# Square root as Exp of half a Ln in the score bound of an attention and expert layer (8 cores of a Trainium2)

## The chip, the cores and the metric

The program runs on the 8 cores of one Trainium2 chip, every core with its own half of one of 4 sequences. Each core has five engines that run their own queues in order: TensorE (PE, matmuls; PEld is its weight load), VectorE (DVE), ScalarE (ACT), GpSimd (POOL) and SyncE (SP). The metric is the device time in microseconds (us) of the slowest core, for one execution.

## The reference

One layer in post-norm order: self-attention with rotary positions over 4 sequences of 2048 tokens, width 2048, 16 heads of 128; then a mixture of 8 experts of which the router picks 2 per token; after both a residual sum and a layer norm. Cut to what matters:

```python
q = rotary(proj(Wq, bq)); k = rotary(proj(Wk, bk)); v = proj(Wv, bv)
attn = softmax(einsum('bhqd,bhkd->bhqk', q, k) * HD ** -0.5)
out = einsum('bhqk,bhkd->bhqd', attn, v)
x = layernorm(x + out @ Wo.T + bo)
w = sigmoid(x @ Wg.T); keep the best 2 of 8, divided by their sum
x = layernorm(x + sum_e w_e * (silu(x @ W1_e.T) * (x @ W3_e.T)) @ W2_e.T)
```

A softmax does not change when the same number is taken off all scores of a row, so any bound on the scores may stand in for their maximum.

## The kernel before, in words

Everything is kept transposed: features on the 128 partitions, tokens along the free dimension. A core has 1024 tokens of its own, and computes keys and values for all 2048 of its sequence.

The attention runs in 8 groups of 2 heads (`emit_group`). A group first makes V for both heads (L292 or L317, copied out by ScalarE at L305 or L324). Then each head goes through the same steps:

- `proj_rope` for Q (2 pieces of 512 tokens) and for K (4 pieces): 16 steps of matmuls each (L397, L403). ScalarE adds the bias (L363, Identity), VectorE squares the result (L368), a matmul with ones sums the squares (L373), and VectorE takes the largest into the small row `msc` (L377, L382, L386). The rotation itself is the "tail" of a piece: a matmul that swaps neighbours (L339) and three VectorE operations (L344, L349, L354).
- `bound_finale`, called after the last K pieces and before their two tails: VectorE multiplies the largest squared norm of Q with that of K (L430), ScalarE takes the square root, scaled (L433), a matmul with a row of ones spreads this one number over the 128 partitions (L436), and VectorE writes its negative into `mq_sb` (L439). It is the bound that the exponentials take off.
- `st_merged`: for each of 16 blocks of 128 keys two score matmuls (L472), one ScalarE exponential over 1024 scores (L479, which reads `mq_sb` as its bias), and four matmuls that sum the exponentials (L451) and weight V with them (L458). TensorE's order is L472 of block 0, L472 of block 1, L451 and L458 of block 0, L472 of block 2, and so on.
- `epilogue_m`: the division by the sum as Ln and Exp on ScalarE (L491, L495), a VectorE product (L499) and the V bias (L503).

After the 8 groups come the output projection (L542) with the residual and the statistics of the first layer norm, the router, the eight experts (L782, L799, L856) and the second layer norm.

The order of the work is that of the code: each engine replays its own list, and `Sched` gives every operation a semaphore wait on the last writer or the readers of what it uses. Operations on the same engine wait on each other in the same way, except on TensorE. The loads of ScalarE's function tables (ACT_TABLE_LOAD) do not stand in the code: they are put in when the program is compiled, and the profile gives them the line of the operation that they stand in front of.

Of the kernel before, what the change touches and what calls it, by code (L numbers as in the profile page):

```python
# [7 lines left out]
AF = mybir.ActivationFunctionType  # L8
# [13 lines left out]
SCALE = float(HD) ** -0.5  # L22
# [101 lines left out]
def build_program(debug=False):  # L124
# [62 lines left out]
    msc = nc.alloc_sbuf_tensor("msc", [1, 8], F32)  # L187
# [26 lines left out]
    def T(fn, r=(), w=()):  # L214
        S_.op("tensor", fn, r, w)

    def V(fn, r=(), w=()):
        S_.op("vector", fn, r, w)

    def A(fn, r=(), w=()):  # L220
        S_.op("scalar", fn, r, w)
# [26 lines left out]
    for dc in range(NDC):  # L248
        G(lambda g, dc=dc: g.dma_start(
            R1_bf.ap()[:, dc * S:(dc + 1) * S], d_x[dc]),  # L250
            r=([f"R1_{dc - 2}"] if dc >= 2 else []),
            w=[f"R1_{dc}"], dma=f"gx{dc % 2}")
# [3 lines left out]
        w=["ws0", "ws1"], dma="swq")  # L256
# [4 lines left out]
        w=["ws2", "ws3"], dma="swk")  # L261
    G(lambda g: g.dma_start(
        wg_sb.ap().rearrange("p (dc e) -> p dc e", dc=NDC), d_wg),
        w=["wg"], dma="gld")
    T(lambda t: t.matmul(pa[0].ap()[:, 0:NE], ones_r_f.ap(), fbrow.ap(),
                         start=True, stop=True),
      r=["ones", "fbrow"], w=["pa0"])
    V(lambda v: v.tensor_copy(fbb.ap(), pa[0].ap()[:, 0:NE]),
      r=["pa0"], w=["fbb"])

    def emit_group(gi):
        if gi > 0:
# [7 lines left out]
                w=["ws0", "ws1"], dma="swq")  # L280
# [4 lines left out]
                w=["ws2", "ws3"], dma="swk")  # L285

        if gi == 0:
            for dc in range(NDC):
                def vmm0(t, dc=dc):
# [13 lines left out]
                  w=[f"pa{b}" for b in range(8)])  # L303
            for tc in range(NDC):
# [3 lines left out]
                    r=[f"pa{tc // 2}"], w=[f"vb{tc}"])  # L308
        else:
            for tc in range(NDC):  # L310
# [3 lines left out]
                def vmm(t, tc=tc, bank=bank):  # L314
# [11 lines left out]
                    r=[pk], w=[f"vb{tc}"])  # L326

        for hl in range(2):
# [100 lines left out]
            def bound_finale():  # L429
                V(lambda v: v.tensor_tensor(  # L430
                    msc.ap()[0:1, 6:7], msc.ap()[0:1, 4:5], msc.ap()[0:1, 5:6],
                    ALU.mult), r=["msc"], w=["msc"])
                A(lambda s: s.activation(msc.ap()[0:1, 7:8], msc.ap()[0:1, 6:7],  # L433
                                         AF.Sqrt, scale=SCALE * SCALE),
                  r=["msc"], w=["msc"])
                T(lambda t: t.matmul(  # L436
                    pa[3].ap()[:, 0:1], ones_r_f.ap(), msc.ap()[0:1, 7:8],
                    start=True, stop=True), r=["msc", "ones"], w=["pa3"])
                V(lambda v: v.tensor_scalar(  # L439
                    mq_sb.ap()[:, 6:7], pa[3].ap()[:, 0:1], -1.0, None,  # L440
                    ALU.mult), r=["pa3"], w=["mq"])

            proj_rope(4, 4096 + hl * 2048, ["ws2" if hl == 0 else "ws3"], bkc,
                      "bkc", ck_sb, sk_sb, kbuf, koff,
                      [f"kb{hl}_{i}" for i in range(4)], finale=bound_finale)

            def st_merged():
# [64 lines left out]
    for gi in range(NH // 2):  # L512
        emit_group(gi)
        if debug and gi == 0:
            Y(lambda s: s.dma_start(d_dbg_qkv[0][:, 0:2 * TL], qbuf.ap()),
              r=["qb0_0", "qb0_1", "qb1_0", "qb1_1"], dma="dbg5")
            Y(lambda s: s.dma_start(d_dbg_qkv[1], kbuf.ap()),
              r=[f"kb{h}_{i}" for h in range(2) for i in range(4)], dma="dbg5")
            Y(lambda s: s.dma_start(d_dbg_qkv[2], vbuf.ap()),
              r=[f"vb{t}" for t in range(NDC)], dma="dbg5")  # L520

    for i in range(NDC):
        V(lambda v, i=i: v.tensor_copy(
            xy.ap()[:, i * TL:(i + 1) * TL], R1_bf.ap()[:, i * S: i * S + TL]),
            r=[f"R1_{i}"], w=[f"xy{i}"])

    if debug:
        Y(lambda s: s.dma_start(d_dbg_ao, aog.ap()),
          r=[f"ao{h}" for h in range(NH)], dma="dbg6")
    pending_stats = [None]  # L530
    for ec in range(NHC):
# [5 lines left out]
            w=[wok], dma=f"swo{sl}")  # L537
# [15 lines left out]
        for nq in range(2):  # L553
# [5 lines left out]
                r=[f"pa{ob + nq}", f"xy{ec}", "boc"], w=[f"R1_{ec}"])  # L559
# [97 lines left out]
    for nq in range(2):  # L657
        V(lambda v, nq=nq: v.tensor_copy(
            scr_f.ap()[0:8, nq * 512:(nq + 1) * 512], pa[nq].ap()[0:8, :]),
            r=[f"pa{nq}"], w=["sf0", "sf1"])  # L660
    for tt in range(8):
# [5 lines left out]
            r=["pa2"], w=["rt"])  # L667
    A(lambda s: s.activation(wr_sb.ap(), rt_sb.ap(), AF.Sigmoid),
      r=["rt"], w=["wr"])
# [4 lines left out]
    for tt in range(8):  # L674
# [26 lines left out]
      r=["m1"], w=["m1"])  # L701
# [180 lines left out]
    for e in range(NE):  # L882
        emit_h13(e, hook=lambda e=e: emit_ew_rows(e))
        emit_w2(e, stats=(e == NE - 1))
        if debug:
            Y(lambda s, e=e: s.dma_start(d_dbg_acc[e], R1_f32.ap()),
              r=[f"R1_{i}" for i in range(NHC)], dma="dbg2")
            Y(lambda s, e=e: s.dma_start(d_dbg_g[e], aog.ap()),
              r=[f"ao{j}" for j in range(NH)], dma="dbg3")
            Y(lambda s, e=e, sl=e % 2: s.dma_start(  # L890
                d_dbg_ewb[e], scr_f.ap()[:, sl * TL:(sl + 1) * TL]),
                r=[f"sf{2 * (e % 2)}", f"sf{2 * (e % 2) + 1}"], dma=f"dbg4{e % 2}")
# [118 lines left out]
```

How the kernel before makes its waits and increments, by code:

```python
    def replay(self, engname, engobj):  # L103
        wm = {}
        for o in self.stream[engname]:
            waits = {}
            for d in o["deps"]:
                if d["cnt"] is None:
                    continue
                val = (self.totals[d["sem"]]
                       if (d["dma"] and d["dma"] in self.batch_sems)
                       else d["cnt"])
                if waits.get(d["sem"], 0) < val:
                    waits[d["sem"]] = val
            wl = [(k, v) for k, v in waits.items() if wm.get(k, 0) < v]
            for k, v in wl:
                engobj.wait_ge(self.handles[k], v)
                wm[k] = v
            inst = o["fn"](engobj)
            if o["marked"]:
                inst.then_inc(self.handles[o["sem"]], 16 if o["dma"] else 1)
# [798 lines left out]
        @block.sync  # L920
        def _(s):
            S_.replay("sync", s)
            s.wait_ge(handles[("dma", "st")], st_total)
```

## Time and profile before

| what | us |
|---|---|
| the two timed runs | 3157.67 and 3518.6 |
| their median | 3338.14 |
| the profiled execution | 3156.6 |
| its span, on the slowest core (core 7) | 3155.1 |
| the spans of the eight cores | 3143.8 to 3155.1 |
| busy in that span: PE | 2631.6 (83%) |
| DVE | 802.7 (25%) |
| ACT | 637.3 (20%) |
| POOL | 172.2 (5%) |

The span runs from the first to the last instruction of the program on the slowest core, and the rows below are of that core. A busy time adds what an engine worked anywhere in the span; it says nothing of who waited. Matmuls are pipelined, so the busy time of PE counts more than the array's work. The granted clock is the share of TensorE's full 2.4 GHz that the chip allowed in a stretch; 0.50 is 1.2 GHz.

### The profile page before, as it was taken

To read this page: it belongs to the slowest core of one execution; us is meant where nothing else is said; L and a number is where in the kernel's file an instruction comes from. 1 tells how busy PE (TensorE), PEld (TensorE's weight loads), DVE (VectorE), ACT (ScalarE), POOL (GpSimd) and SP (SyncE) were. 2 spreads that over 40 slices of the span, in tenths; PEclk is the share of its full clock that TensorE was granted. 3 is DMA by queue.
4 is the path that set the end of the run, shared out by engine and by line. 5 is a ranking of instruction groups with operands and counts; after the bars stand their busy time and mean duration, and the time that the engine had idled before them with its cause. 6 is when DMAs were issued, how large, how long until landed. Compare 5 with 4: busy or idle time off the path is not lost.

```text
span 3155.1 us, 32027 instructions; the slowest of 8 cores (3143.8 to 3155.1 us)
## 1 busy us (share of the span) xinstructions
PE 2631.6 (83%) x12262; PEld 1205.3 (38%) x12262; DVE 802.7 (25%) x1452; ACT 637.3 (20%) x824; POOL 172.2 (5%) x323
## 2 busy tenths in 40 slices
PE   4777777878777777779849999998989999998993
PEld 3234242524243342424314344343434444343441
DVE  0222223121312222222271212213131222213126
ACT  0342424334333324243200000000000000000031
POOL 1000000000000000000000101001010100101000
PEclk9888898988888888989969999999999999999996
DMA  9210101001000101002403444344444444444423
GB/s 152 37 27 14 27 14 27 14 14 26 15 14 14 27 14 27 8 7 47 81 14 67 70 70 74 61 80 61 75 70 70 74 67 77 61 77 62 73 44 117
DMA packets 50726, 155.32 MB, mean 49 GB/s; under 512 B 6162, under 2 KB 6290, under 8 KB 49298
## 3 DMA queue, kind: packets, MB, share of 16 engines
q0 software_dynamic: 47264, 142.69, 27.8%
q1 hardware_dynamic: 3314, 10.59, 0.9%
q8 instruction: 101, 1.65, 0.2%
q14 instruction: 47, 0.39, 0.0%
HBM read 287.54 MB, written 8.39 MB: 94 GB/s over the span
## 4 chain that ended last, share of the span: by engine, by line
PE 73%; DVE 9%; DMA 9%; issue 5%; ACT 4%; DVEq 0%; ACTq 0%; POOL 0%; POOLq 0%
PE pb L782 14%; PE pb L799 14%; PE pb L856 9%; DMA wslab<-w_t 6%; PE pb L317 6%; PE pb L397 6%; PE pb L403 6%; PE pb L451 4%; PE pb L458 3%; PE pb L542 3%; PE pb L472 3%; DMA R_bf<-x_t 2%; PE pb L373 1%; DVE scr_bf L368 1%; ACT scr_bf L479 1%
## 5 line engine op out<-in xcount | busy, mean ns | idle before, releaser
L856 PE MATMUL pb<-aog,wslab 128*128 128x512 bf16 x2048 | 459.6, 380 | 56.1 <-DMA wslab<-w_t 55.5
L782 PE MATMUL pb<-xy,wslab 128*128 128x512 bf16 x2048 | 464.8, 386 | 0.0
L799 PE MATMUL pb<-xy,wslab 128*128 128x512 bf16 x2048 | 452.5, 379 | 0.0
L793 ACT ACTIVATE scr_bf<-pb 128x512 bf16<-128x512 f32 x128 | 69.5, 594 | 1321.3 <-PE pb L782 1321.3
L856 PEld LDWEIGHTS pb<-aog,wslab 128*128 128x128 bf16 x2048 | 194.7, 98 | 317.3 <-issue 97.4
L397 PE MATMUL pb<-R_bf,wslab 128*128 128x512 bf16 x768 | 311.0, 405 | 5.5 <-ACT vbuf L305 5.5
L403 PE MATMUL pb<-R_bf,wslab 128*128 128x512 bf16 x768 | 310.1, 404 | 0.0
L479 ACT ACTIVATE scr_bf<-pb,mq_sb 128x1024 bf16<-128x1024 f32 x256 | 283.4, 1114 | 103.5 <-PE pb L472 103.3
L782 PEld LDWEIGHTS pb<-xy,wslab 128*128 128x128 bf16 x2048 | 202.5, 99 | 251.4 <-issue 19.0
L799 PEld LDWEIGHTS pb<-xy,wslab 128*128 128x128 bf16 x2048 | 200.5, 98 | 241.5
L869 DVE TENSOR_TENSOR R_f<-pb,R_f 128x512 f32<-128x512 f32 x256 | 177.1, 692 | 340.6 <-PE pb L856 327.3
L814 DVE TENSOR_TENSOR scr_bf<-pb,scr_f 128x512 bf16<-128x512 f32 x128 | 88.0, 687 | 646.7 <-PE pb L799 646.7
L451 PE MATMUL pb<-scr_bf,ones_sq 128*128 128x512 bf16 x512 | 205.6, 402 | 26.3 <-ACT scr_bf L479 15.7
L317 PE MATMUL pb<-wslab,R_bf 128*128 128x256 bf16 x1792 | 209.6, 282 | 14.7 <-ACT vbuf L324 14.7
L458 PE MATMUL pb<-scr_bf,vbuf 128*128 128x512 bf16 x512 | 204.8, 400 | 0.0
L373 PE MATMUL pb<-scr_bf,ones_sq 128*128 128x512 bf16 x96 | 41.7, 435 | 192.8 <-DVE scr_bf L368 191.1
L317 PEld LDWEIGHTS pb<-wslab,R_bf 128*128 128x128 bf16 x1792 | 180.7, 101 | 43.9 <-issue 16.5
L472 PE MATMUL pb<-qbuf,kbuf 128*128 128x512 bf16 x512 | 173.9, 425 | 19.2 <-DVE scr_f L344 19.2
L368 DVE TENSOR_TENSOR scr_bf<-scr_bf 128x512 bf16<-128x512 bf16 x96 | 40.4, 420 | 411.4 <-ACT scr_bf L363 411.4
L499 DVE TENSOR_TENSOR aog<-pb,scr_f 128x512 bf16<-128x512 f32 x32 | 22.1, 692 | 431.0 <-ACT scr_f L495 431.0
L363 ACT ACTIVATE scr_bf<-pb,bkc 128x512 bf16<-128x512 f32 x64 | 42.3, 686 | 388.0 <-DVE scr_f L349 219.4
L397 PEld LDWEIGHTS pb<-R_bf,wslab 128*128 128x128 bf16 x768 | 79.5, 103 | 107.4 <-issue 29.8
(116 smaller groups left out, 1585.5 us busy)
## 6 DMA issues: line engine op xcount, KB each, us to landing
wslab<-w_t POOLq DMA_DIRECT2D x128, 512.0 KB, 5.1
wslab<-w_t POOLq DMA_DIRECT2D x128, 256.0 KB, 3.8
wslab<-wv_t POOLq DMA_DIRECT2D x8, 1024.0 KB, 9.0
R_bf<-x_t POOLq DMA_DIRECT2D x16, 512.0 KB, 7.0
wslab<-wq_t POOLq DMA_DIRECT2D x8, 1024.0 KB, 9.4
wslab<-wk_t POOLq DMA_DIRECT2D x8, 1024.0 KB, 9.4
wslab<-wo_t POOLq DMA_DIRECT2D x16, 512.0 KB, 5.0
y<-R_f SPq DMA_DIRECT2D x16, 512.0 KB, 2.6
```

What stands on the lines that cost most here:

```text
L317: last = t.matmul(pa[bank].ap()[:, 0:256], R1_bf.ap()[:, dc * S + tc * 128: dc * S + tc * 128 + 128], wslab.ap()[:, 8192 + dc * 256: 8192 ...
L397: t.matmul(pa[pb[0]].ap(), wslab.ap()[:, wbase + dc * 128: wbase + dc * 128 + 128], R1_bf.ap()[:, dc * S + a * 512: dc * S + a * 512 + 512 ...
L403: return t.matmul(pa[pb[1]].ap(), wslab.ap()[:, wbase + dc * 128: wbase + dc * 128 + 128], R1_bf.ap()[:, dc * S + a * 512 + 512: dc * S + ...
L451: T(lambda t, kc=kc, j=j, qb=qb: t.matmul(pa[6 + qb].ap(), ones_sq.ap(), scr_bf.ap()[:, j * 1024 + qb * 512: j * 1024 + qb * 512 + 512], s ...
L458: T(lambda t, kc=kc, j=j, qb=qb, hl=hl: t.matmul(pa[4 + qb].ap(), vbuf.ap()[:, kc * 256 + hl * 128: kc * 256 + hl * 128 + 128], scr_bf.ap( ...
L472: t.matmul(pa[2 * j + qb].ap(), kbuf.ap()[:, koff + kc * 128: koff + kc * 128 + 128], qbuf.ap()[:, qoff + qb * 512: qoff + qb * 512 + 512] ...
L479: A(lambda s, j=j: s.activation(scr_bf.ap()[:, j * 1024:(j + 1) * 1024], pb[j].ap(), AF.Exp, bias=mq_sb.ap()[:, 6:7], scale=SCALE), r=[f"p ...
L542: last = t.matmul(pa[ob + nq].ap(), wslab.ap()[:, sl * 2048 + dc * 128: sl * 2048 + dc * 128 + 128], aog.ap()[:, dc * TL + nq * 512: dc * ...
L782: last = t.matmul(pa[nc2].ap(), wslab.ap()[:, W1OFF[s1] + dc * 128: W1OFF[s1] + dc * 128 + 128], xy.ap()[:, dc * TL + nc2 * 512: dc * TL + ...
L799: last = t.matmul(pa[4 + nc2].ap(), wslab.ap()[:, W3OFF[s1] + dc * 128: W3OFF[s1] + dc * 128 + 128], xy.ap()[:, dc * TL + nc2 * 512: dc * ...
L856: last = t.matmul(pa[wb + nc2].ap(), wslab.ap()[:, W2OFF[s2] + fc * 128: W2OFF[s2] + fc * 128 + 128], aog.ap()[:, fc * TL + nc2 * 512: fc ...
L869: V(lambda v, hc=hc, nc2=nc2, wb=wb: v.tensor_tensor(R1_f32.ap()[:, hc * TL + nc2 * 512: hc * TL + nc2 * 512 + 512], pa[wb + nc2].ap(), R1 ...
```

## The change

In `bound_finale` the one ScalarE instruction that took the square root becomes two: a Ln with the same scale, and an Exp of half of it, which reads and writes the same single number. exp(ln(x) / 2) is the square root of x. Nothing else is changed. The lines behind it move down by three in the changed kernel.

```diff
                 A(lambda s: s.activation(msc.ap()[0:1, 7:8], msc.ap()[0:1, 6:7],
-                                         AF.Sqrt, scale=SCALE * SCALE),
+                                         AF.Ln, scale=SCALE * SCALE),
+                  r=["msc"], w=["msc"])
+                A(lambda s: s.activation(msc.ap()[0:1, 7:8], msc.ap()[0:1, 7:8],
+                                         AF.Exp, scale=0.5),
                   r=["msc"], w=["msc"])
```

ScalarE's queue in one head before, from the K pieces to the first half of the epilogue (the waits in brackets are the semaphores of the engines named):

```order
L363 ACTIVATE scr_bf<-pb,bkc 128x512 [waits e_tensor,e_scalar,e_vector] x2
L433 ACTIVATE msc<-msc 1x1 [waits e_vector]
L479 ACTIVATE scr_bf<-pb,mq_sb 128x1024 [waits e_tensor,e_vector]
L479 ACTIVATE scr_bf<-pb,mq_sb 128x1024 [waits e_tensor,e_vector,e_scalar]
L479 ACTIVATE scr_bf<-pb,mq_sb 128x1024 [waits e_tensor,e_scalar] x14
L491 ACTIVATE scr_f<-pb 128x512 [waits e_tensor]
L495 ACTIVATE scr_f<-scr_f 128x512 [waits e_scalar]
```

The one ScalarE instruction between the K pieces and the exponentials is L433. Here is the same place in the changed kernel, where L482, L494 and L498 are the L479, L491 and L495 of before:

```order
L363 ACTIVATE scr_bf<-pb,bkc 128x512 [waits e_tensor,e_scalar,e_vector] x2
L433 ACTIVATE msc<-msc 1x1 [waits e_vector]
L436 ACTIVATE msc<-msc 1x1 [waits e_scalar]
L482 ACTIVATE scr_bf<-pb,mq_sb 128x1024 [waits e_tensor,e_vector] x2
L482 ACTIVATE scr_bf<-pb,mq_sb 128x1024 [waits e_tensor,e_scalar] x14
L494 ACTIVATE scr_f<-pb 128x512 [waits e_tensor]
L498 ACTIVATE scr_f<-scr_f 128x512 [waits e_scalar]
```

One instruction is added, the new L436, and it waits for the one in front of it on its own engine. Nothing changes places.

## Rows read from the trace of the kernel before

**Rows 1.** The chain that ended last, share of the span by engine.

```profile
PE 73%; DVE 9%; DMA 9%; issue 5%; ACT 4%; DVEq 0%; ACTq 0%; POOL 0%; POOLq 0%
```

**Rows 2.** ScalarE's groups: count | busy us, mean ns | idle before, until whom.

```profile
L324 ACT CAST vbuf<-pb 128x256 bf16<-128x256 f32 x112 | 40.9, 371 | 149.8 <-PE pb L317 149.8
...
L479 ACT ACT_TABLE_LOAD x16 | 20.5, 1283 | 43.2 <-DVE scr_f L349 43.2
...
L495 ACT ACTIVATE scr_f<-scr_f 128x512 f32<-128x512 f32 x32 | 20.1, 629 | 3.2 <-ACT scr_f L491 0.4
L433 ACT ACT_TABLE_LOAD x15 | 19.2, 1283 | 68.1 <-DVE msc L430 68.1
L491 ACT ACTIVATE scr_f<-pb 128x512 f32<-128x512 f32 x32 | 18.8, 588 | 9.9 <-PE pb L451 9.9
...
L433 ACT ACTIVATE msc<-msc 1x1 f32<-1x1 f32 x16 | 3.2, 202 | 5.3 <-DVE msc L430 5.1
...
L305 ACT ACT_TABLE_LOAD x1 | 1.3, 1283 | 79.5 <-PE pb L292 79.5
```

**Rows 3.** Waits: engine, line <- whom: us in total, times, longest.

```profile
ACT L433 <- DVE msc L430: 68.1, 15, 4.8
...
PE pb L436 <- ACT msc L433: 47.9, 16, 3.1
```

**Rows 4.** Timeline, first head: start, us, engine, line [idle before <- releaser].

```profile
128.39 0.15 DVE L430 TENSOR_TENSOR msc<-msc 1x1 f32<-1x1 f32 x1
128.62 0.20 ACT L433 ACTIVATE msc<-msc 1x1 f32<-1x1 f32 x1 [5.09 <-DVE msc L430]
...
128.97 0.55 PE L436 MATMUL pb<-msc,ones_r_f 1*128 1x1 f32 x2 [1.79 <-ACT msc L433]
```

**Rows 5.** Timeline, second head, from its L430 to its first L451 and L458.

```profile
199.02 0.15 DVE L430 TENSOR_TENSOR msc<-msc 1x1 f32<-1x1 f32 x1
199.25 1.28 ACT L433 ACT_TABLE_LOAD   x1 [4.46 <-DVE msc L430]
200.54 0.20 ACT L433 ACTIVATE msc<-msc 1x1 f32<-1x1 f32 x1
...
200.89 0.55 PE L436 MATMUL pb<-msc,ones_r_f 1*128 1x1 f32 x2 [3.07 <-ACT msc L433]
...
203.43 1.28 ACT L479 ACT_TABLE_LOAD   x1 [2.69 <-DVE scr_f L349]
...
204.09 0.68 DVE L344 TENSOR_TENSOR scr_f<-pb,sk_sb 128x512 f32<-128x512 f32 x1
...
204.73 2.12 ACT L479 ACTIVATE scr_bf<-pb,mq_sb 128x1024 bf16<-128x1024 f32 x2
...
204.92 0.58 PE L472 MATMUL pb<-qbuf,kbuf 128*128 128x512 bf16 x1 [1.20 <-DVE scr_f L344]
...
205.98 0.58 PE L451 MATMUL pb<-scr_bf,ones_sq 128*128 128x512 bf16 x1 [0.47 <-ACT scr_bf L479]
...
206.37 0.63 PE L458 MATMUL pb<-scr_bf,vbuf 128*128 128x512 bf16 x1
...
206.79 0.63 PE L451 MATMUL pb<-scr_bf,ones_sq 128*128 128x512 bf16 x1
```

**Rows 6.** Timeline, second head, Ln and Exp of its epilogue.

```profile
229.47 0.60 ACT L491 ACTIVATE scr_f<-pb 128x512 f32<-128x512 f32 x1 [0.62 <-PE pb L451]
...
230.16 0.63 ACT L495 ACTIVATE scr_f<-scr_f 128x512 f32<-128x512 f32 x1
```

**Rows 7.** Stretches: length, busy PE, PEld, DVE, ACT, POOL (counts), granted clock, DMA share, GB/s.

```profile
818.16:827.17 9.01, 5.62 (x14) 1.95 (x15) 4.03 (x7) 4.89 (x5) 0.00 (x0) 0.50 0.00 0
827.17:848.43 21.26, 20.18 (x89) 7.53 (x88) 0.00 (x0) 16.16 (x15) 0.00 (x0) 1.00 0.00 1
1164.75:1175.33 10.58, 7.18 (x17) 2.40 (x18) 4.04 (x8) 5.78 (x6) 0.00 (x0) 0.50 0.00 0
1175.33:1195.79 20.46, 19.23 (x85) 7.28 (x84) 0.00 (x0) 15.26 (x15) 0.00 (x0) 1.00 0.00 1
```

## The prediction

> **What bounds the kernel now.** I read the chain of work that ended last first, then the ScalarE groups, then the waits, then the timeline of two heads. The chain's summary gives PE 73% of the span and ACT 4% [rows 1]: TensorE sets the time, and ScalarE counts only where TensorE stands still for it. The ScalarE groups show where the changed line matters [rows 2]: an ACT_TABLE_LOAD of 1283 ns belongs to L433 15 times and to L479 16 times, one pair in each of the 16 heads, except that the first head has no L433 load. So ScalarE loads the table that has Sqrt, runs one 1x1 Sqrt of 202 ns, and loads another table for the softmax exponentials. Nothing else loads a table inside the attention: Ln (L491) and Exp (L495), the copies (L324) and the biased Identity (L363) run between these loads without one. L305's single load, before the first head, is the table in which the first Sqrt is already found. In all, 31 loads stand in the attention, 20.5 + 19.2 = 39.7 us of ScalarE time; what they are worth is decided by who waits for them.
>
> The waits [rows 3] say that TensorE stood 47.9 us before L436 until ACT L433, 16 times, 3.1 us the longest. That stretch begins while VectorE still reduces the maxima, so not all of it is the load. Two heads part the two: the first head runs the same chain without a load. There L430 starts at 128.39, the Sqrt at 128.62 and L436 at 128.97, which is 0.58 us from L430 to L436 [rows 4]. In the next head L430 starts at 199.02, the load at 199.25, the Sqrt at 200.54 and L436 at 200.89, which is 1.87 us [rows 5]. The L433 load costs the chain 1.87 - 0.58 = 1.29 us, its full length: ScalarE's queue waits for L430 first and loads after it.
>
> **The change, part by part.** (a) Sqrt becomes Ln. Ln and Exp follow each other at L491 and L495 with no load between them, and the second starts 0.09 us after the first ends (229.47 + 0.60 to 230.16) [rows 6]. If one table with Ln, Exp, Identity and the copy is in place from L305 on, the 15 loads of L433 go, and nothing in this chain hides them: 1.29 us a head. A 1x1 Ln I price like the 1x1 Sqrt, 202 ns [rows 2], so the swap itself is worth nothing.
>
> (b) The Exp is added. It needs the Ln's result and lies on the same chain in front of L436, with 202 ns for the instruction and 0.09 us for the wait between dependent ScalarE operations: 0.29 us a head, in all 16. Bounds: 0.20 us if the two overlapped fully at the seam, 0.72 us if the Exp took as long as L495's 128x512 one (629 ns + 0.09) [rows 2]; I take 0.29, because the 1x1 row is the same size. Behind the Ln and the Exp on ScalarE's queue stands only L479's first exponential, which needs L472's scores, and these are behind L436 on TensorE anyway. On TensorE the two swap products L339 and all of L472 queue behind L436; on VectorE the L344 to L354 tail queues behind L439. So the whole head moves with L436.
>
> (a) and (b) together: 1.29 - 0.29 = 1.00 us earlier in 15 heads, 0.29 us later in the first.
>
> (c) The 16 loads in front of L479's first exponential go too. This one is partly covered. In [rows 5] the load runs from 203.43 to 204.71, the first two exponentials follow from 204.73, and TensorE's L451 starts at 205.98 when the first is done. Without the load the first exponential would start at 203.43 and end some 1.06 us later (two take 2.12), near 204.5. But L451 stands behind the fourth L472 in TensorE's order, and that starts at 204.92, released by VectorE's L344 (L344 of 204.09 frees the bank that it writes). Matmuls there start 0.42 us apart (L458 at 206.37, L451 at 206.79), so L451 can start at 204.92 + 0.42 = 205.34 at the earliest. The gain is 205.98 - 205.34 = 0.64 us, not 1.28; what is late next is VectorE's L344. Bounds: 0 if something else holds L451, 1.28 if L472 too came forward. I take 0.64 in each of 16 heads.
>
> Raw sum: 15 x (1.00 + 0.64) + (0.64 - 0.29) = 24.6 + 0.35 = 24.95 us, say 25.0.
>
> (d) TensorE's clock takes part of this back. Around each of these stalls the granted clock is 0.50 (1.2 GHz), and it comes back to full only some way into the score loop. Two heads show what the moment of return is worth [rows 7], each followed from the end of L430 to the end of its last L458. In one, the half-speed stretch lasts 9.01 us and the full-speed rest 21.26, 30.27 in all; in the other 10.58 and 20.46, 31.04 in all. So 1.57 us more of half speed costs 0.77 us, about half. If the clock returns at the same moment as now although the work starts earlier, the work pulled forward runs at half speed and only about half of the 25.0 is kept, 12.5 us. If the return moves with the work, all 25.0 stay. Nothing in the trace of before fixes which; it will differ from head to head as the heads shift against these moments. I take the middle, 18.8 us. The Trainium skill (TensorE: Matmul & The Clock Gate, Part 1) says that the monitor behind this clock runs freely and is not started by the work, which speaks against the full gain. By that rule alone, in a head whose return stays put, the sum would be 12.5; by the row alone either end is possible.
>
> (e) A second rule of the Trainium skill (ScalarE: Activation LUTs, What ACT_TABLE_LOAD costs) makes a switch dearer: about 2.66 us, of which 1283 ns are the load and the rest a drain. The load agrees with the 1283 ns of [rows 2]; the drain is not seen, since the chain with a load is longer by 1.29 us in all. By the page's price the 15 switches at L433 would be worth another 15 x 1.37 = 20.6 us, and the time would be 3117.2. TensorE's wait leaves no room for it: the first head's 1.79 us [rows 4] taken 16 times and 15 x 1.29 for the loads make 48.0 us, and 47.9 were measured [rows 3]. So the rows decide, and this case gets no chance of its own.
>
> The rest of the program (projection of the output, both layer norms, the eight experts) keeps its instructions and merely starts earlier.
>
> The profiled execution took 3156.6 us for a span of 3155.1; the sum is made against the former: 3156.6 - 18.8 = 3137.8. Of the two timed runs the lower, 3157.67, agrees with it within 1.1 us; the median, 3338.14, is the middle between it and a run of 3518.6, and is not what the forecast is compared with.
>
> **The rivals.** (1) Everything removed counts: the L479 load in full, the clock moving with the work. 15 x (1.00 + 1.28) + 0.99 = 35.2, so 3121.4. For it: the load does lie straight in front of the exponential. Against it: the fourth L472, which waits for VectorE [rows 5].
> (2) The L479 load turns out to be worth nothing and the clock keeps half of the rest: (15 x 1.00 - 0.29) / 2 = 7.4, so 3149.2. For it: L472's wait for L344 ends 0.2 us after the load does. Against it: L451 starts 0.64 us after L472 would let it.
> (3) The other side: Ln and Exp are served from different tables. Then each head keeps a load in front of the Ln, gets a second 1.28 us load between Ln and Exp, and loses only the one before L479: 1.28 + 0.29 - 0.64 = 0.93 us worse per head, 14.9 us over 16, so 3171.5. It decides as soon as one load stands between the two 1x1 instructions. For it: the trace of before never shows this short pair. Against it: L491 and L495 alternate 32 times without a load [rows 2, 6], and 15 us is the most that it costs.
> (4) The change doesn't do what it says: the loads at L433 and L479 stay as they are, because the first table is chosen for another function, and only the Exp is added: 16 x 0.29 = 4.6 us, so 3161.2.
>
> **How the numbers follow.** My forecast 0.72, rival 1 0.09, rival 2 0.12, rival 3 0.05, rival 4 0.02. The forecast's own ends are 3131.6 (all of 25.0) and 3144.1 (half of it). To leave out no more than 2 in 10, the range reaches down near rival 1 and up to rival 2: 3122 to 3149. A change of 2% is 63 us, about what a measurement of this kernel can tell from none; the largest case here is 35 us. So within 2% gets 0.96; 0.02 on either side is for what shifts later, such as the waits for expert weights.
>
> **What would show it.** Right: of the loads in the attention only that of L305 remains; the new pair takes about 0.2 us each with no gap above 0.1; the wait of TensorE for the new Exp falls from 47.9 us to about 47.9 - 15.00 + 0.29 = 33.2; the first exponential starts as soon as its two score products are done; L451 follows the fourth L472 without a gap. Wrong: any load between the 1x1 instructions (rival 3), a gap in front of L451 that remains (c), or heads that end 1.64 us earlier each with no part given back, or less than half of it (d).

## The result, and the profile after

| | before | changed |
|---|---|---|
| timed executions, median | 3204.34 (18 runs) | 3138.44 (19 runs) |
| ratio, with its 95% interval | | 0.9912 [0.9887, 0.9936] |
| once more, beside the last experiments | 3162.64 (11 runs) | 3141.18 (6 runs), 0.9938 [0.9924, 0.9951] |
| profiled execution | 3156.6 | 3135.5 |
| spans of the eight cores, mean | 3150.7 | 3131.6 |

Some executions of either kernel come out up to 12% longer at a lower granted clock on a part of the cores; they are in the medians, and the ratios are taken without them.

The changed kernel is faster, by 0.6 to 0.9%. The two intervals share 0.9924 to 0.9936, which is 20 to 24 us, and the profiled executions are 21.1 us apart. The gain was forecast as 18.8 us of 3156.6, a ratio of 0.9940, which lies just outside the first interval and inside the second. The time itself came within 0.6 us of the forecast (3138.44 against 3137.8), which is luck: the section on why the prediction was right or wrong names the errors that cancel in it.

The chain that ended last, by engine, in the changed kernel:

```profile
PE 73%; DVE 9%; DMA 9%; issue 6%; ACT 3%; DVEq 0%; ACTq 0%; POOL 0%; POOLq 0%
```

ScalarE's share falls from 4% to 3% [rows 1]. Its groups (line, engine, operation, count | busy us, mean ns | idle before, until whom):

```profile
L433 ACT ACTIVATE msc<-msc 1x1 f32<-1x1 f32 x16 | 3.2, 202 | 73.8 <-DVE msc L430 73.8
L436 ACT ACTIVATE msc<-msc 1x1 f32<-1x1 f32 x16 | 3.2, 202 | 1.5
...
L305 ACT ACT_TABLE_LOAD x1 | 1.3, 1283 | 82.3 <-PE pb L292 82.3
L671 ACT ACT_TABLE_LOAD x1 | 1.3, 1283 | 45.4 <-DVE rt_sb L668 45.4
L796 ACT ACT_TABLE_LOAD x1 | 1.3, 1283 | 7.0 <-PE pb L785 7.0
L608 ACT ACT_TABLE_LOAD x1 | 1.3, 1283 | 6.2 <-DVE scr_f L604 6.2
```

The 31 loads at L433 and L479 of [rows 2] are gone. One load at L305 serves all of the attention, and the three others stand outside it. The new Exp (L436) takes the same 202 ns as the Ln, and ScalarE idles 1.5 us before it in all, 0.09 us each time: no load between the two.

The waits that answer to [rows 3]:

```profile
ACT msc L433 <- DVE msc L430: 73.8, 16, 5.0
...
PE pb L439 <- ACT msc L436: 33.5, 16, 2.1
...
PE pb L475 <- DVE scr_f L344: 19.2, 16, 1.2
```

TensorE's wait for the bound falls from 47.9 to 33.5 us; 33.2 was forecast. The wait that now holds the first sum, L475 for VectorE's L344 (the L472 of before), is 19.2 us in 16 heads. The second head in order of time, against [rows 5] (the slowest core is now core 3, so the clock of the rows is shifted):

```profile
197.62 0.15 DVE L430 TENSOR_TENSOR msc<-msc 1x1 f32<-1x1 f32 x1
197.86 0.20 ACT L433 ACTIVATE msc<-msc 1x1 f32<-1x1 f32 x1 [4.47 <-DVE msc L430]
198.16 0.20 ACT L436 ACTIVATE msc<-msc 1x1 f32<-1x1 f32 x1
...
198.50 0.55 PE L439 MATMUL pb<-msc,ones_r_f 1*128 1x1 f32 x2 [2.09 <-ACT msc L436]
...
201.06 1.11 ACT L482 ACTIVATE scr_bf<-pb,mq_sb 128x1024 bf16<-128x1024 f32 x1 [2.70 <-DVE scr_f L349]
...
201.71 0.68 DVE L344 TENSOR_TENSOR scr_f<-pb,sk_sb 128x512 f32<-128x512 f32 x1
...
202.54 0.59 PE L475 MATMUL pb<-qbuf,kbuf 128*128 128x512 bf16 x1 [1.20 <-DVE scr_f L344]
...
202.91 0.63 PE L454 MATMUL pb<-scr_bf,ones_sq 128*128 128x512 bf16 x1
...
203.34 0.63 PE L461 MATMUL pb<-scr_bf,vbuf 128*128 128x512 bf16 x1
```

From L430 to the spreading matmul it is 0.88 us (198.50 - 197.62) where it was 1.87. The first exponential starts at 201.06 with no load in front of it, when VectorE's L349 releases it, and L454 follows the fourth score product after 0.37 us (202.54 to 202.91), where L451 started 1.06 us behind it before. From L430 to the first sum it is 5.29 us, where it was 6.96.

For the comparisons below I use three numbers, each a mean over the eight cores. S adds up, over the 16 heads, the time from the start of L430 to the start of the first sum of exponentials: it is the part that the edits change directly. T is the time from the end of the first L430 to the first matmul of the output projection: all of the attention from the first head's bound on. H is the time in T at half clock, added up from the granted clock of the trace. Each comes from one traced execution of a kernel. Before: S 110.3, T 1307.6, H 304.0. Changed: S 84.7, T 1285.3, H 283.6; traced once more, beside the last experiments, it gave 84.7, 1285.4 and 284.6. So S fell by 25.6 us and T by 22.3. The mean span fell by 19.1: what lies before and behind T is 3.2 us longer, of which 2.7 are the eight experts and the layer norm behind them (1536.1 to 1538.8, with single cores between 1529.6 and 1541.0 in the two traces). That part has the same code in all kernels, and it took between 1535.9 and 1539.3 us in the other traces without extra matmuls, so the 2.7 us lie within its spread and are not shown to be a cost of the change.

### The profile page after: what moved, and what is told of

It reads as the page before. It is cut to its first block, busy times and chain, and to the rows that moved or that the text cites. A ratio compares the mean times of both kernels' runs of the same rounds, so it can differ in the third digit from the quotient of the medians.

```text
span 3134.0 us, 32012 instructions; the slowest of 8 cores (3128.2 to 3134.0 us)
## 1 busy us (share of the span) xinstructions
PE 2629.3 (84%) x12262; PEld 1206.9 (39%) x12262; DVE 802.2 (26%) x1452; ACT 602.5 (19%) x809; POOL 172.3 (5%) x323
## 4 chain that ended last, share of the span: by engine, by line
PE 73%; DVE 9%; DMA 9%; issue 6%; ACT 3%; DVEq 0%; ACTq 0%; POOL 0%; POOLq 0%
PE pb L785 14%; PE pb L802 14%; PE pb L859 9%; DMA wslab<-w_t 6%; PE pb L397 6%; PE pb L403 6%; PE pb L317 6%; PE pb L454 4%; PE pb L475 4%; PE pb L461 4%; PE pb L545 4%; DMA R_bf<-x_t 2%; DVE scr_f L344 1%; PE pb L373 1%; DVE scr_bf L368 1%
## 5 line engine op out<-in xcount | busy, mean ns | idle before, releaser
L482 ACT ACTIVATE scr_bf<-pb,mq_sb 128x1024 bf16<-128x1024 f32 x256 | 285.1, 1114 | 163.7 <-PE pb L475 119.7
L454 PE MATMUL pb<-scr_bf,ones_sq 128*128 128x512 bf16 x512 | 209.5, 409 | 18.8 <-ACT scr_bf L482 9.5
L317 PE MATMUL pb<-wslab,R_bf 128*128 128x256 bf16 x1792 | 202.9, 276 | 15.3 <-ACT vbuf L324 15.3
L373 PE MATMUL pb<-scr_bf,ones_sq 128*128 128x512 bf16 x96 | 41.9, 437 | 192.7 <-DVE scr_bf L368 191.1
L317 PEld LDWEIGHTS pb<-wslab,R_bf 128*128 128x128 bf16 x1792 | 177.4, 99 | 41.1 <-issue 17.0
L475 PE MATMUL pb<-qbuf,kbuf 128*128 128x512 bf16 x512 | 177.0, 432 | 19.2 <-DVE scr_f L344 19.2
L397 PEld LDWEIGHTS pb<-R_bf,wslab 128*128 128x128 bf16 x768 | 79.0, 103 | 103.4 <-issue 25.0
L403 PEld LDWEIGHTS pb<-R_bf,wslab 128*128 128x128 bf16 x768 | 79.0, 103 | 101.4 <-issue 20.5
```

What stands on the lines that cost most here:

```text
L317: last = t.matmul(pa[bank].ap()[:, 0:256], R1_bf.ap()[:, dc * S + tc * 128: dc * S + tc * 128 + 128], wslab.ap()[:, 8192 + dc * 256: 8192 ...
L397: t.matmul(pa[pb[0]].ap(), wslab.ap()[:, wbase + dc * 128: wbase + dc * 128 + 128], R1_bf.ap()[:, dc * S + a * 512: dc * S + a * 512 + 512 ...
L403: return t.matmul(pa[pb[1]].ap(), wslab.ap()[:, wbase + dc * 128: wbase + dc * 128 + 128], R1_bf.ap()[:, dc * S + a * 512 + 512: dc * S + ...
L454: T(lambda t, kc=kc, j=j, qb=qb: t.matmul(pa[6 + qb].ap(), ones_sq.ap(), scr_bf.ap()[:, j * 1024 + qb * 512: j * 1024 + qb * 512 + 512], s ...
L475: t.matmul(pa[2 * j + qb].ap(), kbuf.ap()[:, koff + kc * 128: koff + kc * 128 + 128], qbuf.ap()[:, qoff + qb * 512: qoff + qb * 512 + 512] ...
L482: A(lambda s, j=j: s.activation(scr_bf.ap()[:, j * 1024:(j + 1) * 1024], pb[j].ap(), AF.Exp, bias=mq_sb.ap()[:, 6:7], scale=SCALE), r=[f"p ...
```

## The experiments

**The load in front of the exponentials alone (e1_hoist).** The kernel before, with one instruction more:

```diff
...
+                A(lambda s: s.activation(dum.ap(), ones_r_f.ap()[0:1, 0:1], AF.Exp),
+                  r=["ones"], w=["dum"])
```

> The kernel before, with one more ScalarE instruction, a 1x1 Exp into an unused number, right behind the Sqrt and off the chain: the load of the exponentials' table then falls into ScalarE's wait for the scores, while the Sqrt keeps its own load on the chain. This is part (c) alone. Measure: from the start of the first L430 to that of the last, mean of the eight cores (1277.2 us before, 1255.4 after). Theory (c), 0.64 us in each of 15 heads, 9.6 us raw: 1267.6 if all of a shift is kept, 1270.0 if three quarters, 1272.4 if the clock keeps half. Rival, that load is hidden behind VectorE anyway: 1277. Rival, it counts in full (1.28): 1258.

Ratio 0.9988 [0.9951, 1.0025]. From the first to the last L430 1273.8 us, a smaller gain than even the case in which half is kept; S 99.2, T 1304.1, H 308.7. The timeline of its second head (lines are one or three further down than before):

```profile
198.66 0.15 DVE L431 TENSOR_TENSOR msc<-msc 1x1 f32<-1x1 f32 x1
198.89 1.28 ACT L434 ACT_TABLE_LOAD   x1 [4.67 <-DVE msc L431]
200.18 0.20 ACT L434 ACTIVATE msc<-msc 1x1 f32<-1x1 f32 x1
200.40 1.28 ACT L437 ACT_TABLE_LOAD   x1
...
200.53 0.55 PE L439 MATMUL pb<-msc,ones_r_f 1*128 1x1 f32 x2 [3.08 <-ACT msc L434]
...
201.70 0.20 ACT L437 ACTIVATE dum<-ones_r_f 1x1 f32<-1x1 f32 x1
...
203.09 1.11 ACT L482 ACTIVATE scr_bf<-pb,mq_sb 128x1024 bf16<-128x1024 f32 x1 [1.19 <-DVE scr_f L350]
...
204.56 0.59 PE L475 MATMUL pb<-qbuf,kbuf 128*128 128x512 bf16 x1 [1.20 <-DVE scr_f L345]
...
204.94 0.63 PE L454 MATMUL pb<-scr_bf,ones_sq 128*128 128x512 bf16 x1
```

The load behind the Sqrt now stands at 200.40, beside the spreading matmul, and nobody waits for it. The first exponential starts when VectorE's L350 (the L349 of before) releases it (203.09), and the first sum is held by the fourth score product (204.56) as part (c) said: S falls by 11.1 us, 0.69 per head for the 0.64 of (c). Yet T falls by 3.5 only. H rose by 4.7.

**The chain alone (e4_chain_only).** The changed kernel, with a 1x1 Sqrt off the chain behind the Exp, which brings the load in front of the first exponential back:

```diff
...
+                A(lambda s: s.activation(dum.ap(), ones_r_f.ap()[0:1, 0:1], AF.Sqrt),
+                  r=["ones"], w=["dum"])
```

> The changed kernel with one more ScalarE instruction, a 1x1 Sqrt into an unused number behind the Exp and off the chain: the chain to the spreading matmul stays short as in the changed kernel, but the load in front of the first exponential is back. This is parts (a) and (b) without (c), the other half of e1_hoist. The stretch from the start of L430 to the first sum of exponentials, added over 16 heads, was 110.3 us before, 99.2 in e1_hoist and 84.7 in the changed kernel; here 95.5 is expected. Measure: first L430 to the output projection, mean of the cores: 1307.6 before, 1304.1 in e1_hoist, 1285.3 in the changed kernel. If a fixed share of a shift is kept (87%, as between before and changed): 1294.7. If what is kept depends on where the heads come to lie against the moments at which the clock returns, there is no such share, and anything between 1303 and 1288 can come (the 31% of e1_hoist to the 126% of f1_late_spread).

Ratio 0.9964 [0.9952, 0.9977]. S 95.9 as expected, T 1297.0, H 295.0: 10.6 of 14.4 us kept, neither the 87% nor an extreme. The two halves alone are worth 3.5 and 10.6 us of T, 14.1 together; both at once are worth 22.3. The parts do not add up, though their S does (11.1 + 14.4 = 25.5, and 25.6 together).

**A longer chain (e2_pad4, e3_pad12).** The changed kernel with four or twelve more 1x1 instructions on the chain:

```diff
+                for _ in range(4):              # 12 in e3_pad12
+                    A(lambda s: s.activation(msc.ap()[0:1, 7:8], msc.ap()[0:1, 7:8],
+                                             AF.Identity), r=["msc"], w=["msc"])
```

> The changed kernel with four more 1x1 Identity instructions on the chain between the Exp and the spreading matmul. Each is 0.20 us and a wait of 0.09 as the Exp was priced, so 1.16 us a head and 17.4 us over the 15 heads between the first and the last L430 (1255.4 us in the changed kernel, mean of the cores). If a shift of the work is kept whole: 1272.8. If three quarters, as part (d) chose: 1268.5. If half: 1264.1. It tests the price of (b) per instruction too: L430 to the spreading matmul should grow by 1.16 us.

> The same with twelve Identity instructions, 3.48 us a head, 52.2 us over the 15 heads, more than one step of the moments at which the clock returns. If a shift is kept whole in the mean: 1307.6. Three quarters: 1294.6. Half: 1281.5.

Ratios 1.0025 [1.0015, 1.0034] and 1.0112 [1.0095, 1.0129]. From first to last L430 1274.7 and 1311.6 us. S grew by 18.8 and 56.9, T by 19.8 and 59.2: about all of the delay arrives, and the even share of three quarters fails. In e2_pad4 one core lifts the mean: core 0 took 1316.3 us in T, the seven others 1303.3 to 1303.6, which is 18.2 longer than the changed kernel. TensorE's wait in e2_pad4:

```profile
PE pb L442 <- ACT msc L440: 52.2, 16, 3.3
```

It was 33.5, so 16 x 4 instructions cost 18.7 us there, 0.29 each, the price of part (b).

**Without the Exp (e5_no_exp).** The changed kernel less its second instruction.

```diff
-                A(lambda s: s.activation(msc.ap()[0:1, 7:8], msc.ap()[0:1, 7:8],
-                                         AF.Exp, scale=0.5),
-                  r=["msc"], w=["msc"])
```

> The changed kernel without the added Exp: the bound is then the Ln alone, so the exponentials and the output are not the reference's; the instructions are otherwise the same. It prices part (b) by itself. L430 to the spreading matmul, 0.88 us in the changed kernel, should fall to 0.59, as in the first head of before, and the 16 stretches from L430 to the first sum by 4.7 us (84.7 to 80.0). First L430 to the output projection, 1285.3 in the changed kernel: 1280.6 if all of it is kept, 1283 if half; by the sum of half the change of these stretches and half the change of the half-speed time in between (283.6 us in the changed kernel), which met all runs so far within 1.2 us, whatever that half-speed time turns out to be.

```profile
PE pb L436 <- ACT msc L433: 28.8, 16, 1.8
```

The Exp costs 33.5 - 28.8 = 4.7 us of TensorE's wait, and S is 80.0, 4.7 less, as expected. T is 1277.6: 7.7 us less for 4.7 taken away, more than the case in which all is kept (1280.6). H is 275.0, 8.6 less. Ratio to before 0.9916 [0.9899, 0.9932].

**The bound spread later (f1_late_spread).** The two swap products L339 go in front of the spreading matmul, which takes a bank of its own, and VectorE's negation goes between the two tails (shortened, with comments added):

```diff
-                emit_tail(nt - 2)
-                emit_tail(nt - 1)
...
+                    emit_tail(nt - 2, "t")
+                    emit_tail(nt - 1, "t")
+                    spread()                    # the matmul of L436, into pa[5]
+                    emit_tail(nt - 2, "v")
+                    neg()                       # VectorE's L439
+                    emit_tail(nt - 1, "v")
...
```

> The changed kernel with the spreading matmul behind the two swap products in TensorE's order, into another bank, and VectorE's negation between the two tails, so that the tails of K run while ScalarE works on the bound. L430 to the first L454-like sum of exponentials was 5.14 us; VectorE's L344 of the second tail, which holds the fourth score product, can start some 1.5 us earlier, so about 3.6 us and 1.5 x 15 = 23 us raw from first to last L430: 1232 if the shift is kept whole, 1238 at three quarters, 1244 at half. Rival: TensorE's wait for ScalarE was covered by VectorE's tails anyway: 1255.

Ratio 0.9836 [0.9821, 0.9850]. From first to last L430 1228.5 us, more than the whole shift. S 61.0, T 1255.4, H 247.1: S fell by 23.7 against the changed kernel, T by 29.9. Its second head:

```profile
196.06 0.15 DVE L442 TENSOR_TENSOR msc<-msc 1x1 f32<-1x1 f32 x1
196.16 0.69 DVE L348 TENSOR_TENSOR scr_f<-pb,sk_sb 128x512 f32<-128x512 f32 x1
...
196.59 0.20 ACT L448 ACTIVATE msc<-msc 1x1 f32<-1x1 f32 x1
...
196.94 0.55 PE L453 MATMUL pb<-msc,ones_r_f 1*128 1x1 f32 x2 [1.24 <-ACT msc L448]
...
198.17 0.15 DVE L458 TENSOR_SCALAR mq_sb<-pb 128x1 f32<-128x1 f32 x1
198.24 0.68 DVE L348 TENSOR_TENSOR scr_f<-pb,sk_sb 128x512 f32<-128x512 f32 x1
198.61 2.30 ACT L499 ACTIVATE scr_bf<-pb,mq_sb 128x1024 bf16<-128x1024 f32 x2 [1.82 <-PE pb L492]
...
199.06 0.58 PE L492 MATMUL pb<-qbuf,kbuf 128*128 128x512 bf16 x1 [0.18 <-DVE scr_f L348]
...
199.87 0.58 PE L471 MATMUL pb<-scr_bf,ones_sq 128*128 128x512 bf16 x1 [0.22 <-ACT scr_bf L499]
```

VectorE's L348 (the L344 of before) starts 0.10 us behind L442 (the L430), beside ScalarE's Ln and Exp, and the first sum comes 3.81 us behind the start of L442 (3.66 behind its end, from which the expected 3.6 was counted).

**Two moves more (f2_scores_first).** In f1_late_spread, the first two score products go ahead of the spreading matmul and both L344 products ("swap" below) ahead of the negation:

```diff
+                for qb in range(2):             # the scores of block 0, then
+                    T(lambda t, ...: t.matmul(pa[qb].ap(), ...))
                 T(lambda t: t.matmul(pa[5].ap()[:, 0:1], ones_r_f.ap(), ...))
...
+                    emit_tail(nt - 2, "swap")
+                    emit_tail(nt - 1, "swap")
                     neg()
```

> f1_late_spread with two more moves: TensorE's first two score products go in front of the spreading matmul, and VectorE's two L344 products go in front of the negation, so that the fourth score product no longer waits for the whole first tail. L430 to the first sum was 3.81 us in f1_late_spread and should come to about 3.1, as the first exponential then starts some 1.9 us behind L430 and takes 1.1: 16 x 0.7 = 11 us less in these stretches (61.0 to 50). First L430 to the output projection, 1255.4 in f1_late_spread: 1244 if all is kept, 1250 if half. If the first exponential waits for something else, 1255.

Ratio 0.9807 [0.9792, 0.9821], the fastest kernel of the study that adds no work; its median is 3100.45 us against 3162.64 for before. S 48.9 (50 expected), T 1248.1, H 245.1: 7.3 of 12.1 us kept. Two of its waits:

```profile
ACT scr_bf L510 <- DVE mq_sb L469: 17.0, 16, 1.1
...
PE pb L464 <- ACT msc L453: 6.2, 16, 0.4
```

TensorE's wait for the bound, 47.9 us before and 33.5 in the changed kernel, is 6.2.

**Extra matmuls that hold the clock (w1_warm_before, w2_warm_after, w3_warm_late).** To the kernel before, the changed one and f1_late_spread, matmuls are added in front of the L373 products and of the spreading matmul:

```diff
+    def warm(n):
+        def wmm(t):
+            for i in range(n):
+                last = t.matmul(pa[5].ap(), ones_sq.ap(), R1_bf.ap()[:, 0:512],
+                                start=True, stop=True)
+            return last
+        if n:
+            T(wmm, r=["R1_0", "ones"], w=["pa5"])
...
+                    warm(18 if nq == 2 else 6)
...
+                warm(8)
```

The 8 in front of the spreading matmul are those of w2_warm_after; w1_warm_before has 12 and w3_warm_late 2.

> The kernel before, with extra matmuls on ones whose result nobody reads, into a free bank, in the stretches in which TensorE waits in a head: 18 in front of the third L373 of K, 6 in front of each other L373, 12 in front of the spreading matmul. They are there to keep TensorE's clock at full through the head. If the half-speed clock costs what the comparison of the runs says (about half of the work's length in half-speed stretches), some 3 to 5 us a head go: first L430 to the output projection 1307.6 falls to about 1230 to 1260. If the extra matmuls only lie in the way, it rises by up to 16 x 2 = 32.

> The changed kernel with the same extra matmuls (8 in front of the spreading matmul, whose wait is shorter). Against w1_warm_before this is the change without the clock: with the clock full in both, the difference of the two from first L430 to the output projection should equal the difference of their stretches from L430 to the first sum of exponentials within 2 us, that is all of it is kept, some 28 us (1.0 us for the chain and about 0.85 for the load in front of the exponentials in each head, where matmuls at full clock stand 0.22 us apart). If a shift is given back for another reason than the clock, less than 24.

> f1_late_spread with the extra matmuls (2 in front of the spreading matmul): both gains in one kernel. If they add, f1_late_spread's 1255.4 us from first L430 to the output projection falls by what w2_warm_after gains over the changed kernel, by an estimate 40 to 70 us. If f1_late_spread already took most of what the clock costs, by under 30.

T is 1252.4, 1219.7 and 1211.4 us, S 97.8, 75.6 and 57.8. The stretch T of w2_warm_after on its slowest core (length, busy us of PE, PEld, DVE, ACT, POOL with counts, granted clock, DMA share, GB/s):

```profile
128.95:1350.92 1221.97, 1117.56 (x5741) 554.20 (x5823) 307.32 (x593) 447.54 (x581) 14.18 (x22) 0.99 0.11 19
```

The granted clock there is 0.99. That the half-speed clock costs the attention tens of us is shown: 55 us go from before to w1_warm_before, although it has more matmuls. But the clean comparison failed: in w1_warm_before 71.3 us of T are still at half clock and in w2_warm_after 29.0, so the two differ by 32.7 us for 22.2 of S. The profiled executions are 3118.79, 3085.04 and 3071.72 us. The ratios are 0.9857 [0.9842, 0.9872] for w1_warm_before and 0.9721 [0.9706, 0.9736] for w3_warm_late; none came out for w2_warm_after. Over all their executions the medians of w2_warm_after and w3_warm_late are 3233.25 and 3252.61 us against 3162.18 for before, so I do not call them an improvement. The experts and the layer norm behind them, with the same code, took 1547.3 to 1549.7 us in these three against 1536.1 before; what the extra matmuls do there was not tried. The gains of f1_late_spread and of the matmuls add only in part: 1255.4 falls by 44.0 us, within the 40 to 70 expected, but the changed kernel's T falls by 65.6.

## Why the prediction was right or wrong

**Parts (a), (b), (c) and their sum: right.** The 15 loads at L433 were on the chain in full (1.87 to 0.88 us, 0.99 a head against 1.00 forecast), the Exp costs 0.29 (e2_pad4 and e5_no_exp measure it twice), and the load in front of the first exponential is worth 0.69 (e1_hoist) instead of 0.64, held by VectorE's L344 as named. The raw sum was 25.0; S fell by 25.6. One sign did not hold: the first exponential does not start with its score products but when VectorE's L349 releases it, as [rows 5] showed already. It cost nothing, since the fourth score product comes later. Taking the load off the chain gave 0.99 + 0.29 = 1.28 us, its own length. The further drain that the Trainium skill (ScalarE: Activation LUTs, What ACT_TABLE_LOAD costs) counts with a switch shows nowhere here.

**Part (d), what the clock gives back: the step that failed.** It said that half to all of the shift is kept, took the middle, 75%, and looked for the clock's answer only in the stretch around the bound. Measured: 22.3 of 25.6 us, 87%, 3.5 us more than the forecast 18.8. T splits into the heads (from the start of each L430 to the end of its last sum of exponentials; 493.4 us before, 475.3 changed) and what lies between them (814.2 and 810.0). The heads kept 18.1 us, 71%: there the middle was close. The other 4.2 us were gained between the heads, where the time at half clock fell from 80.2 to 69.1 us a core; (d) put any change there at nothing. So the term was mis-sized by what it left out, and its two ends were wrong too, as the other pairs of kernels show:

| from, to | S | H | T | (S + H) / 2 | T / S | T in the heads | T between them |
|---|---|---|---|---|---|---|---|
| before, e1_hoist | -11.1 | +4.7 | -3.5 | -3.2 | 32% | -10.0 | +6.5 |
| before, e4_chain_only | -14.4 | -9.0 | -10.6 | -11.7 | 74% | -11.1 | +0.5 |
| before, changed | -25.6 | -20.4 | -22.3 | -23.0 | 87% | -18.1 | -4.2 |
| changed, e5_no_exp | -4.7 | -8.6 | -7.7 | -6.7 | 164% | -6.8 | -0.9 |
| changed, e2_pad4 | +18.8 | +20.0 | +19.8 | +19.4 | 105% | +12.2 | +7.6 |
| changed, e3_pad12 | +56.9 | +59.9 | +59.2 | +58.4 | 104% | +57.4 | +1.8 |
| changed, f1_late_spread | -23.7 | -36.5 | -29.9 | -30.1 | 126% | -36.9 | +7.1 |
| f1_late_spread, f2_scores_first | -12.1 | -2.0 | -7.3 | -7.1 | 60% | -6.7 | -0.5 |
| w1_warm_before, w2_warm_after | -22.2 | -42.3 | -32.7 | -32.3 | 147% | -39.8 | +7.1 |

There is no fixed share: the same kind of edit keeps a third of its time in one place and half as much again in another. The column (S + H) / 2 is bookkeeping. Time at half clock is stall plus work, and work there takes twice as long (in the second head of before, whose half-speed stretch ends at 209.36, 128x512 matmuls start 0.42 us apart at half clock, 208.93 to 209.35, and 0.22 apart at full, 209.57 to 209.79; the lines follow). So a change costs its stall and half of the change in work done at half clock, which is (H - S) / 2. It meets T within 1.1 us in all nine pairs, and so nothing but the stall and the clock is needed to explain T. One trace shows the same with no edit at all: in e2_pad4, core 0 has the S of the other seven within 0.1 us, 26.3 us more H than core 1, and 12.7 us more T, nearly all of it between the heads. So T differs by some us between cores that run the same instructions, and a share of a small shift such as e5_no_exp's 4.7 us is rough. The sum is not a forecast, since H is known only from the trace of the new kernel.

```profile
208.93 0.60 PE L458 MATMUL pb<-scr_bf,vbuf 128*128 128x512 bf16 x1
209.35 0.39 PE L451 MATMUL pb<-scr_bf,ones_sq 128*128 128x512 bf16 x1
209.57 0.38 PE L458 MATMUL pb<-scr_bf,vbuf 128*128 128x512 bf16 x1
209.79 0.59 PE L472 MATMUL pb<-qbuf,kbuf 128*128 128x512 bf16 x2
```

How the clock gives back and adds is seen in the second head. Here is the half-speed stretch around the bound in the kernel before (columns as in [rows 7]):

```profile
195.71:209.36 13.65, 7.38 (x18) 2.37 (x19) 6.21 (x13) 5.39 (x6) 0.00 (x0) 0.50 0.34 59
```

In the changed kernel, with the stretches around it:

```profile
185.00:194.62 9.62, 4.81 (x22) 1.91 (x20) 4.46 (x8) 1.37 (x2) 0.71 (x1) 1.00 0.21 37
194.62:208.27 13.65, 9.15 (x22) 3.28 (x23) 5.96 (x13) 3.75 (x5) 0.00 (x0) 0.50 0.34 53
208.27:220.00 11.73, 11.58 (x50) 4.21 (x49) 0.00 (x0) 9.06 (x9) 0.00 (x0) 1.00 0.00 0
```

In e1_hoist:

```profile
194.42:208.07 13.65, 7.51 (x18) 2.61 (x19) 6.37 (x14) 5.40 (x7) 0.00 (x0) 0.50 0.30 60
208.07:220.00 11.93, 11.60 (x52) 4.33 (x51) 0.00 (x0) 9.38 (x9) 0.00 (x0) 1.00 0.00 0
```

And in f1_late_spread:

```profile
191.66:201.90 10.24, 6.58 (x15) 2.07 (x16) 6.39 (x14) 2.63 (x4) 0.00 (x0) 0.50 0.56 95
```

The stretch is 13.65 us long in all three of the first kernels: in the changed kernel the stall got shorter, the stretch did not, and TensorE ran 22 matmuls in it instead of 18. The four more cost about 0.2 us each, out of the 1.67 us that this head gained. In f1_late_spread the stretch is 10.24 us and holds 15 matmuls. All heads of all cores (8 x 16) together, from the granted clock in the traces:

| kernel | half-speed stretch around the bound, us | other half-speed stretches in T |
|---|---|---|
| before | 13.65 in 106 heads, 17.07 in 22 | 188 |
| e1_hoist | 13.65 in 128 | 206 |
| e4_chain_only | 13.65 in 128 | 188 |
| changed | 13.65 in 128 | 160 |
| e5_no_exp | 13.65 in 115, 10.24 in 13 | 154 |
| e2_pad4 | 13.65 in 128 | 204 |
| e3_pad12 | 17.07 in 128 | 169 |
| f1_late_spread | 10.24 in 128 | 204 |
| f2_scores_first | 10.24 in 128 | 200 |

Two things decide what a shorter stall is worth. The first is the stretch around the bound, which had one of three lengths and did not slide along with the work by the tenths of a us that an edit moves it. What its end is worth is what (d) read off two heads: in the 120 heads of before (the first of each core left out) it ends 9.16 to 12.64 us behind L430 though the instructions are the same, and the head lasts 0.47 us longer for each us (0.49 in [rows 7]). The 98 of them with a stretch of 13.65 us last on average 1.01 us longer than the 120 of the changed kernel, all at 13.65, for a stall that is 1.67 longer: where the length stays, a part is given back. Where the length falls, more than the stall comes out: in f1_late_spread 2.30 us for 1.48 against the changed kernel, in the 13 heads of e5_no_exp 1.34 us for 0.29. Part (d) had only the first case and the even shift.

The second is the other half-speed stretches, which all lie between the heads, behind TensorE's waits at L373 (the sums of squares) and at L317 (V of the next group). The change did away with 28 of them; f1_late_spread has 44 more than the changed kernel, e1_hoist 18 more than before. That is why e1_hoist kept 10.0 of its 11.1 us in the heads and only 3.5 in T. Why they become more or fewer is not shown.

The Trainium skill (TensorE: Matmul & The Clock Gate, Part 1) says that the monitor behind the clock runs freely and does not restart with the kernel. That the stretch ends anywhere between 9.16 and 12.64 us behind the same instruction agrees. The 12.5 us that the prediction drew from this rule, for returns that stay put, did not come: the heads alone kept 18.1.

**What was put at nothing outside T.** The prediction let the rest of the program merely start earlier. What lies outside T came out 3.2 us longer in the traced pair, within its spread as said above. With 3.5 us more gained in T this leaves 22.3 - 3.2 = 19.1 us less in the mean span, so the close time is two errors that cancel, and luck.

**What a measurement can tell.** The prediction held 2%, 63 us, to be about what can be told from no change, and gave 0.96 to staying within it. The intervals reach only 0.25 and 0.14% to either side, so a gain of 0.6% is clear of none, and these chances said nothing of it.

**The rivals.** (1) fell: the load in front of the exponentials is worth 0.69 of its 1.28 us. (2) fell as it was put, since that load is worth something in S; in T e1_hoist alone looks like it, because of the half-speed stretches between the heads. (3) and (4) fell: no load is left at L433, L436 or L482.

**What stays open.** Which heads get which length of stretch, and how many half-speed stretches fall between the heads, was not forecast for any kernel here; both are known only from the traces.

## What to carry to other kernels

Look for two functions from different tables in a loop: here every head but the first paid two loads, one for each change of function. What such a load is worth is read at the engine that waits: here in full on the chain between two engines, and in part where another wait ended next. What a shorter stall is worth where TensorE's clock is at half varied from 32 to 164% of its length here, so compare S, H and T instead of one time, look between the heads too, and test parts together, since their T does not add. The order of the work was worth more than the swap of functions: with the spreading matmul behind independent work, TensorE's wait for the bound fell from 33.5 to 6.2 us, and the time of the kernel to 0.9807 of before.

## What was not expected of the hardware

The ScalarE load at L433 started only when VectorE's L430 had ended (199.02 + 0.15 to 199.25), although ScalarE had been idle for 4.46 us, so the chain paid its whole length. A 1x1 instruction of the same function as the exponentials, put off the chain, pulled their load 2.7 us forward into idle time (from 203.43 - 199.02 = 4.41 us behind L430 to 200.40 - 198.66 = 1.74). And the half-speed stretch around the bound was 10.24, 13.65 or 17.07 us long, and nothing else, in all heads of nine kernels, however the stalls inside it were changed.
